# The 2 MB weight stores and reloads are begun by ScalarE instead of SyncE

## The reference

```
ln_out = LN(x)
q  = LN(fp8lin(ln_out, wq));   k = LN(fp8lin(ln_out, wk));   v = fp8lin(ln_out, wv)      # 16 / 8 / 8 heads of 128
qx = LN(fp8lin(ln_out, wqx));  kx, vx = split(ctx @ w_kv_x)                               # 16 / 8 / 8 heads
core = softmax(q k^T / sqrt(128)) v;   xout = softmax(qx kx^T / sqrt(128)) vx
x1 = x + tanh(g_xattn) * proj(fp8(concat(core, xout)))
out = x1 + tanh(g_ffn) * w_down(quant8(silu(gate) * up)),  gate, up = w_gate_up(quant8(LN(x1)))
```

## Time and profile before

| | us |
|---|---|
| median of 3 runs | 2029.78 (2028.43 to 2035.61) |
| the profiled execution | 2037.14 |
| its span in the trace | 2035.4 |
| VectorE busy | 1747.3 (86%) |
| TensorE busy | 1677.8 (82%) |
| ScalarE busy | 1186.9 (58%) |
| GpSimd busy | 1017.2 (50%) |

### The profile page before, as it was taken

The page is one execution under the profiler, slowest core; times in us unless marked ns, Lnnn a source line. Parts: engine busy times, 40 slices in busy tenths (PEclk is TensorE's granted clock), DMA queues, the critical chain, the costliest instruction groups (busy, mean ns, idle before and its releaser), DMA issues.

```text
span 2035.4 us, 34986 instructions
## 1 busy us (share of the span) xinstructions
PE 1677.8 (82%) x11147; PEld 1020.8 (50%) x11164; DVE 1747.3 (86%) x4062; ACT 1186.9 (58%) x2963; POOL 1017.2 (50%) x1327
## 2 busy tenths in 40 slices
PE   1467777767999988889998878898999967999996
PEld 0344444444566655556565545555666623444442
DVE  5768889897999989999998899999998964777774
ACT  2024555545788887778787666667777861222221
POOL 3566567665666656676665555555665631000000
PEclk7678999888999999999999999999999988999997
DMA  2235666666898988889988877889997697423200
GB/s 85 90 115 143 145 158 137 143 148 166 190 215 197 224 206 202 177 188 214 201 200 187 176 163 181 194 214 212 204 182 154 126 231 225 117 74 103 73 17 16
DMA packets 632027, 325.45 MB, mean 160 GB/s; under 512 B 547744, under 2 KB 590880, under 8 KB 626720
## 3 DMA queue, kind: packets, MB, share of 16 engines
q1 hardware_dynamic: 631840, 323.16, 67.6%
HBM read 140.61 MB, written 48.23 MB: 93 GB/s over the span
## 4 chain that ended last, share of the span: by engine, by line
DVE 44%; PE 28%; DMA 12%; POOL 7%; issue 7%; ACT 2%; SPq 1%; POOLq 0%; DVEq 0%; ACTq 0%
DVE pp L943 8%; DMA pt<-pp 8%; DVE nmx L933 8%; PE psum L682 5%; PE psum L640 4%; PE psum L657 4%; PE psum L628 4%; PE psum L600 4%; PE psum L699 3%; PE psum L607 3%; DMA raw<-in_w 3%; DVE xh L916 2%; DVE wbt L821 2%; POOL raw L1348 2%; DVE ast L902 1%
## 5 line engine op out<-in xcount | busy, mean ns | idle before, releaser
L628 PE MATMUL psum<-qk 128*128 128x512 f16 x1536 | 429.8, 390 | 71.4 <-DVE pp L943 69.3
L600 PE MATMUL psum<-wbt,xqt 128*128 128x256 f16 (+1 forms) x4096 | 421.6, 255 | 50.8 <-DVE xh L916 35.3
L600 PEld LDWEIGHTS psum<-wbt,xqt 128*128 128x128 f16 x4096 | 340.7, 102 | 167.3 <-DVE xh L916 40.1
L1231 ACT ACTIVATE psum<-psum,nmx 128x512 f32<-128x512 f32 x512 | 340.6, 665 | 143.7 <-DVE nmx L933 138.6
L943 DVE SCALAR_TENSOR_TENSOR pp<-psum,prs,pp 128x512 f16<-128x512 f32 x512 | 378.2, 739 | 31.0 <-ACT pp L1242 31.0
L1242 ACT ACTIVATE pp<-psum,prs 128x512 f16<-128x512 f32 x512 | 350.7, 685 | 62.5 <-DMA pt<-pp 62.4
L933 DVE TENSOR_REDUCE nmx<-psum 128x1 f32<-128x512 f32 x512 | 343.4, 671 | 26.9 <-PE psum L628 26.0
L1237 ACT ACTIVATE prs<-psm 128x1 f32<-128x1 f32 x512 | 107.4, 210 | 250.4 <-DVE psm L938 248.5
L640 PE MATMUL psum<-pt,vs 128*128 128x512 f16 x768 | 208.5, 396 | 52.7 <-ACT cy L1250 28.2
L1424 POOL TENSOR_TENSOR qk<-y,qk 128x512 f16<-128x512 f32 x192 | 233.3, 1215 | 16.0
L628 PEld LDWEIGHTS psum<-qk 128*128 128x128 f16 x1536 | 144.3, 100 | 162.7 <-DVE pp L943 74.0
(11 more groups left out here) (169 smaller groups left out, 2795.1 us busy)
## 6 DMA issues: line engine op xcount, KB each, us to landing
wbt<-ws SPq DMA_DIRECT2D x24, 2048.0 KB, 9.0
ws<-wbt SPq DMA_DIRECT2D x8, 2048.0 KB, 7.7
catd<-cy SPq DMA_DIRECT2D x64, 256.0 KB, 2.7
raw<-in_wgu SPq DMA_DIRECT2D x64, 256.0 KB, 3.2
wbt<-catd SPq DMA_DIRECT2D x8, 2048.0 KB, 9.8
raw<-in_w SPq DMA_DIRECT2D x32, 384.0 KB, 3.8
pt<-pp SPq DMA_TRANSPOSE x512, 3.3
raw<-in_wp SPq DMA_DIRECT2D x32, 256.0 KB, 3.3
```

The source lines that it names most:

```text
L600: ins = e.matmul(bank[:, o0:o0 + c1 - c0], xv[:, v, kt * 512 + tt * 128:kt * 512 + (tt + 1) * 128], wb[i][:, h, kt, c0:c1], start=kt == 0 ...
L628: ins = e.matmul(SB(n), qk[i][:, jq, u, ss], qk[i][:, jk, w, :], start=k == 0, stop=k == 2)
L1231: e.activation(SB(n), SB(n), ACT.Exp, bias=nmx[:, k], accum_out=psm[:, k]).then_inc(s["exp"], 1)
```

## The change

The two functions `store_w` and `load_w` move, unchanged, from SyncE's program to ScalarE's. They are then begun on ScalarE's own transfer queue. In ScalarE's loop they stand behind `v_hi` and ahead of `head_y`; the reload stands two slots later than before (n + 6 for n + 8, so at n = 16 nw - 38), the stores at the same n. The first store moves to the first loop step of ScalarE.

```
@@ sp_program
-            def store_w(it):
-                q.wait_ge("w_dn", it * 5 + 5)
-                e.dma_start(ws[it], wbt[:, it % 2, :]).then_inc(s[f"w_st{it % 2}"], 16)
-
-            def load_w(it):
-                q.wait_ge("gb", (it - 1) * 4)
-                q.wait_ge(f"w_st{it % 2}", 16 * (NG // 2))
-                e.dma_start(wbt[:, it % 2, :], ws[it % NG]).then_inc(s[f"w_ld{it % 2}"], 16)
...
             load_raw(0, 4)
-            store_w(0)
             load_raw(1, 0)
...
                     turn(n - 3)
-                nw, j = divmod(n + 8 + 2 * SLOTS, SLOTS)
-                if j == 0 and NG <= nw < NIT:
-                    load_w(nw)
...
                 for it in kv_at(n - 2, "lo"):
-                    store_w(it)
                     if it + 1 < NG:
                         load_raw(it + 1, 1)
@@ act_program
+            def store_w(it): (as above)
+            def load_w(it): (as above)
...
                     if half == 1:
                         v_hi(it, tt)
+                nw, j = divmod(n + 6 + 2 * SLOTS, SLOTS)
+                if j == 0 and NG <= nw < NIT:
+                    load_w(nw)
+                for it in [0] * (n == FIRST) + kv_at(n - 2, "lo"):
+                    store_w(it)
                 for it, o in heads_at(n):
                     head_y(it, o)
```

More of the change, by code:

```diff
@@ L1201, in act_program, with store_w, load_w @@
             e = q.e
+            def store_w(it):
+                q.wait_ge("w_dn", it * 5 + 5)
+                e.dma_start(ws[it], wbt[:, it % 2, :]).then_inc(s[f"w_st{it % 2}"], 16)
+            def load_w(it):
+                q.wait_ge("gb", (it - 1) * 4)
+                q.wait_ge(f"w_st{it % 2}", 16 * (NG // 2))
+                e.dma_start(wbt[:, it % 2, :], ws[it % NG]).then_inc(s[f"w_ld{it % 2}"], 16)
             def x_turned(b, kt, v):
```

## The result

The changed kernel took 2054.55 us in the median of 5 runs (2047.59 to 2056.27), against 2029.78 before. The profiled execution has a span of 2050.0 us.

A forecast was written before the change was run, and what follows sets the result against it. VectorE was taken to set the pace, waiting for transposes queued behind reloads. The terms -13.9, -4 and +4.6 sum to -13.3 us, so 2029.8 becomes 2017 us, with 2002 to 2042 for 8 in 10.

The forecast's parts named there:

- What bounds the kernel, and what the reloads cost it: Longest stage, 470 to 1690 us: VectorE sets the pace; reloads holding transposes in SyncE's queue cost it 17.4 us.
- Reloads leave the queue of the transposes, -13.9: SyncE's queue: with reloads gone, transposes land sooner; four fifths of the 17.4 us won, 13.9 us.
- The reload gets slower, 11 to 14 us; the place costs 0: ScalarE's queue: reloads land in 11 to 14 us and start two slots later, hidden by 13 slots of cover; cost 0.
- Stores leave the queue of the raw loads, -4; first store 0.3: SyncE's queue: raw loads no longer stand behind stores, 4 us won, including 0.3 from the first store not holding SyncE.
- The starts on ScalarE, +4.6: ScalarE's loop: beginning 24 reloads at 0.57 us each takes 13.7 us, a third of it uncovered, costing 4.6 us.
- A: Rival, transfer engines: packets taken in turn let large ones crowd out small, transposes held as long; 2034 us, chance 0.27.
- B: Rival, ScalarE: held some 2.6 us while beginning each reload, so the kernel gets slower; 2060 us, chance 0.14.
- C: Rival, VectorE: more is won, since late transposes also reach it through TensorE's scores and products; 1995 us, chance 0.13.

The follow-up runs named there:

- e10: Kernel before with stores begun by ScalarE, each reload cut into 8 pieces of 256 KB in SyncE's queue, one behind each of 8 transposes; ratio 0.9860, 2003.7 us.
- e1: Kernel before with only the 8 stores begun by ScalarE, the reloads staying with SyncE at n + 8; ratio 0.9946 to the kernel before.
- e2: Kernel before with only the 24 reloads begun by ScalarE, in their old place n + 8, stores staying with SyncE; ratio 1.0072 to the kernel before.
- e4: Kernel before with 24 additional transfers of 2 KB begun by ScalarE at n + 6; ratio 1.0019 to the kernel before.
- e13: Changed kernel with its reloads at the old place n + 8, still begun by ScalarE; ratio 1.0041 to the kernel before.
- e5: Changed kernel with `ws` laid out in blocks, meant to move runs of 512 B; ratio 1.0174 to the kernel before.
- e8: Changed kernel with `ws` laid out so that runs of 512 B lie 1 KB apart in HBM; ratio 1.0061 to the kernel before.
- e12: e10 with the two last 2 MB loads also cut into 8 pieces each, behind the last 16 transposes; ratio 0.9807 to the kernel before, 1995.99 us.

## Why the prediction was wrong, step by step

*What bounds the kernel, and what the reloads cost it.* Right. The reloads hold the transposes: e10, which takes this away, wins 0.9% over e1, 17 us, where 17.4 was read off the windows. With both intervals it is anything from 12 to 23 us, so that the two numbers are so near is in part luck.

*Reloads leave the queue of the transposes, -13.9.* This is the step that failed. That four fifths of the 17.4 us would go, since a transpose would get about half of the engines' time beside a reload, was my estimate; no run shows this term. In its place the runs show that the transposes get next to nothing at first (one packet under 512 B in the 3 us from 1482.1 us on), then equal numbers of packets, 48 to 47. A row of 16 KB against a packet of 256 B (1152 packets under 512 B with 0.29 MB, 1491 to 1492 us) then gives the reload over nine tenths of the bytes, and 96.7% of the engines' time against 2.7%. A transpose behind a reload was to land within 5 us and took 10.4. In place of -13.9 us, moving the reloads cost 33 us: the changed kernel's 1.0108 against e1's 0.9946. At the old place it costs 15 us (e2).

*The reload gets slower, 11 to 14 us; the place costs 0.* Both wrong. The 11 to 14 us were an estimate that no run shows: it landed in 9.6 us in the median, against 9.0 before. The place costs 0.3% in the old queue and 0.7% in the new one. I had asked only whether the weights come in time (they have 13 slots of (1541.1 - 478.2) / 23 / 16 = 2.9 us), and they do: the trace has no wait of TensorE for a reload. I had not asked which slot's transposes are caught.

*Stores leave the queue of the raw loads, -4; first store 0.3.* Right, but the size is too small: e1 measures 0.54%, 11 us (7 to 15). I had bounded it by VectorE's direct wait of 7.5 us. Up to the first reload VectorE is idle 86.9 us before and 78.2 in e1; 7.5 of these 8.7 us are the direct wait. Where the rest of the 11 us comes from, no trace shows.

*The starts on ScalarE, +4.6.* Right: e4 gives 0.19%, 4 us (1 to 7), with 0.33 us for a start and not 0.57.

*Two terms together.* e1's 0.9946 times e2's 1.0072 is 1.0018; measured 1.0041 (e13). The place brings it to 1.0108.

*The rivals.* A had the mechanism and the reason, the packets' sizes, and 27 in 100. The counts 48 to 47, 366 to 368 and 672 to 675 agree with its packets in turn; the 39 to 105 from 1482.1 us on do not. That a transpose is held as long as before, as A said, is what the 10.5 and 10.6 us show. That one begun just ahead is held too came true for those begun 0.3 us ahead, 3 of 24. Of the small packets A let 8 pass on an engine during a reload, 128 in all: beside 119 of the 144 packets of the reload begun at 1481.08 us, 61 under 512 B did (1482.1 to 1488.5 us). A's price, 2034, was still too low: it had nothing for the place, and nothing for three reloads of 24 that took 13.4, 18.7 and 20.1 us, and the transposes with them. The first of the 24 was begun 5.9 us behind a 2 MB store in ScalarE's queue, where before it stood ahead of the store; the other two each had a transpose begun 0.3 us ahead. Here is the one at 993.38 us:

```profile
993.07 16.18 SPq L386 DMA_TRANSPOSE pt<-pp  x2
...
993.38 0.33 ACTq L1196 DMA_DIRECT2D wbt<-ws  x1
1012.63 0.69 ACT L1237 ACTIVATE pp<-psum,prs 128x512 f16<-128x512 f32 x1 [11.73 <-DMA pt<-pp]
```

A transpose is begun 0.3 us ahead of the reload and misses its reader by 11.7 us. Before, no reload took over 10.2 us. Why these three took so long is open: a third reload with a transpose 0.3 us ahead took 9.1 us. B named 2060 us, the number nearest to 2054.55, but that is luck: its mechanism is refuted by the starts of 0.33 us and by e4. C is refuted by the sign.

## What to carry to other kernels

Do not expect that a large transfer gives way to small ones because it has a queue of its own: where both queues had packets under way here, they shared by packets and not by time (48 to 47 packets in 2 us, with 96.7% and 2.7% of the engines' time). Count how many packets each side has and how large they are. Look also at what is begun within a fraction of a microsecond ahead of the large transfer: here three transposes begun 0.3 us ahead were held too (9.9 to 19.5 us to landing), where those begun 1.4 us ahead or more were not, except beside a store. If small urgent transfers are late behind a large one, cut the large one up and place the pieces between them (here 0.9860 in e10 and 0.9807 in e12); a second queue helped here with the stores (0.9946 in e1) and cost with the reloads (1.0072 in e2).

## What was not expected of the hardware

- Packets of two queues passed one for one even between 16 KB and under 512 B (48 to 47 in 2 us), but only from some 4 us behind the beginning of the reload on (39 to 105 in the 3 us before).
- Runs of 512 B on one side only were put together to packets of 2 KB in a load (366 packets for 0.75 MB, e5); with the runs 1 KB apart in HBM they stayed 512 B (672 for 0.34 MB, e8).
- Beginning a transfer took 0.33 us on ScalarE, for 2 KB (e4) as for a 2 MB reload with rows of 16 KB, where SyncE took 0.57 for the same reload; with the runs of 512 B of e8 it took 0.53 us on ScalarE (medians).
- With the reloads in ScalarE's queue two loads of 2 MB took twice their time (20.1 and 18.7 us against 9.6); the cause is open.
